# An adjacency built from one-hot products: the first two chunks' low one-hots made on the scalar engine, sixteen window ranges per register load, root products in two halves, and a scale chain spread over the attention loop

## The chip, the cores and the metric

The kernel runs as one program on one core of a Trainium2 chip. The metric is the device time of the whole program in microseconds (us), lower is better. TensorE multiplies matrices (PE in the rows, its weight loads are PEld), VectorE is DVE, ScalarE is ACT, GpSimd is POOL, and SyncE (SP) issues most of the transfers. Each engine has its own instruction stream. Its sequencer takes the instructions one by one, waits on semaphores, and does the register arithmetic.

## The reference

Two layers over a graph of 2500 nodes with 256 features and 80000 edges (sorted by destination). Each layer adds a graph convolution and an attention, then a feed-forward part. The parts that the change touches are the edge sums of layer 0 and the attention of layer 1:

```python
def _sage(x, src, dst, W_l, b_l, W_r):
    msg_sum = segment_sum(x[src], dst, N_NODES)
    cnt = segment_sum(ones, dst, N_NODES)
    return (msg_sum / maximum(cnt, 1.0)[:, None]) @ W_l.T + b_l + x @ W_r.T
h_fwd = _sage(x, src, dst, W_l_f, b_l_f, W_r_f)      # layer 0, both directions
h_bwd = _sage(x, dst, src, W_l_b, b_l_b, W_r_b)
...
# layer 1: linear attention with instance-normed k and v; its output joins x
```

## The kernel before

The kernel does the edge sums as dense matrix products. In `graph_stage` it first builds the adjacency matrix A (how many edges go from each source to each destination) out of one-hot vectors, and multiplies it with the projected features while it is being built.

The edges are cut into 625 **chunks** of 128. The destinations are cut into 80 **windows** of 32 nodes (`NW`), four to a **tile** of 128 (`XW`, index `x`; `t` is the tile, 0 to 19). Since the edges are sorted by destination, each window meets a run of chunks. The first two (`FQ`) have buffers of their own: `first_onehot_key` (`fok`, 640 columns a chunk) and `first_onehot_low` (`fol`, 128 columns a chunk). The rest come in **groups** of four (`Q`), with `onehot_key` (`ohk`) and `onehot_low` (`ohl`). Low windows have many edges, high ones few: window 0 takes 18 groups, windows 15 to 39 mostly 2, and from window 46 on each takes 1. How many groups a window has, and at which chunk it begins, is data. Both are packed into one integer of the row `ranges`, and each engine reads it into registers.

The work of one window by engine:

- DVE: the low one-hots of the first two chunks (L607), a register load of four windows' ranges every fourth window (L366, `fetch_tile`), two first keys (L611); then, for each group, four keys (L599) and two low one-hots for two chunks each (L603). A key waits until TensorE has used the one before it in the same buffer, four keys back.
- TensorE: four matmuls for the first chunks (L815), the same register load every fourth window (L366), then eight matmuls for each group (L804). After them come five transposes (L848) and five forward products (L857) for the tile before. In windows with `x == RT` (2) of tiles 0 to 5, eight matmuls follow for two tiles of the root product `x @ W_r` (`roots`, L762).
- ACT: a register load of the next window's range (L362), the source numbers shifted by the next window's offset (L671, `shift`), then the copies out of the PSUM banks: the last window's block of A turned (L697) and straight (L707), and in every fourth window the forward sums (L712).

Two windows' results have banks of their own (`x % 2`), so TensorE can't begin a window before ACT has copied the one two back. ACT may begin window `w`'s part only when DVE has made the low one-hots of all windows before it.

The other place is `linear_attention_stage`. It loops over 20 tiles. TensorE makes k and v (`kv`, L2871, two tiles ahead), ACT squares them, DVE turns the squares into a scale (L2979 to L2985) and scales k (L2988), and TensorE adds k and v into a 64x64 block for each head (`dots`, L2880). Ahead of this loop stands a short chain that scales the next stage's weights `sg_w`: ACT squares the weights (L2932), TensorE sums the squares (L2888), DVE takes the largest (L2968, L2969), ACT its root (L2935), and DVE scales (L2971 to L2975). GpSimd adds a bias to `X` in 20 instructions (L2857) from the stage's start.

## Time and profile before

| what | value |
|---|---|
| time, median of 3 | 1829.48 us (1828.7 to 1834.03) |
| the profiled execution's own time | 1833.38 us, its span 1831.6 us |
| TensorE busy | 1674.0 us, 91% |
| VectorE busy | 966.3 us, 53% |
| ScalarE busy | 669.4 us, 37% |
| granted TensorE clock, mean | 0.961 of full |
| edge windows (first L607 to last) | 47.9 to 434 us |
| linear attention stage | 1403 to 1543 us |

The span counts from the first to the last instruction. Shares of the span say little here, since stages with different limits follow each other. Each stage is read by itself.

### The profile page before, as it was taken

Reading aid. Unit: us, or ns where it says so; the run is one execution under the profiler, and the core shown is the slowest. Engines: PE = TensorE matmul, PEld = TensorE weight load, DVE = VectorE, ACT = ScalarE, POOL = GpSimd, SP = SyncE. Lnnn points to the kernel's source line nnn. Section 1 sums busy time; section 2 is a strip of 40 time slices with the busy share of each in tenths; the row PEclk is TensorE's granted clock in tenths of the full one; section 3 lists DMA queues with packets and bytes.
Section 4 is the critical chain, followed back from the end, with each engine's and each line's share of the span. In section 5 each row is a group of like instructions: output and inputs, shape, how many; then the busy total and the mean of one; then the engine's idle time right before and its main releaser. Section 6 shows DMA issues by size and latency. Waiting matters only on the chain. (4 is left out here: it accounts for less than half of the span.)

```text
span 1831.6 us, 31389 instructions
## 1 busy us (share of the span) xinstructions
PE 1674.0 (91%) x9423; PEld 1104.4 (60%) x9424; DVE 966.3 (53%) x2821; ACT 669.4 (37%) x1352; POOL 235.8 (13%) x290
## 2 busy tenths in 40 slices
PE   6889888987979899999799899999997989998998
PEld 5344555665747423333656799999955557644657
DVE  7888889887568664244511100000055874345862
ACT  3112444674024576665121344444321432201220
POOL 2100000001010003900044000000065000500002
PEclk8999999999989999999599999999998999999989
DMA  2000121225750000000513312211121002141001
GB/s 85 0 15 29 59 87 67 107 116 194 236 155 7 1 1 1 1 1 1 188 58 115 132 66 90 84 63 66 63 84 34 1 1 82 58 145 42 1 1 60
DMA packets 86409, 118.86 MB, mean 65 GB/s; under 512 B 6789, under 2 KB 72511, under 8 KB 86177
## 3 DMA queue, kind: packets, MB, share of 16 engines
q1 hardware_dynamic: 80992, 106.53, 17.2%
q0 software_dynamic: 3936, 10.37, 1.8%
q8 instruction: 55, 0.90, 0.2%
q10 hardware_dynamic: 1376, 0.66, 0.1%
q14 instruction: 50, 0.40, 0.1%
HBM read 70.66 MB, written 46.87 MB: 64 GB/s over the span
## 5 line engine op out<-in xcount | busy, mean ns | idle before, releaser
L804 PE MATMUL bank<-onehot_key,onehot_low 128*128 128x320 bf16 x1304 | 223.4, 303 | 38.2 <-DVE onehot_low L603 23.8
L599 DVE TENSOR_SCALAR onehot_key<-iota_keys,edge_keys 128x640 bf16<-128x640 f16 x652 | 231.5, 381 | 27.5 <-PE bank L804 22.7
L804 PEld LDWEIGHTS bank<-onehot_key,onehot_low 128*128 128x128 bf16 x1304 | 104.3, 99 | 147.9 <-DVE onehot_key L599 55.0
L2647 ACT ACTIVATE hidden<-bank,b_cols 128x128 f32<-128x128 f32 x344 | 126.4, 367 | 178.2 <-PE bank L2574 154.7
L2728 DVE TENSOR_TENSOR slot_columns<-bank,b_rows 128x256 f32 x43 | 18.3, 425 | 290.3 <-PE bank L2580 290.3
L2574 PEld LDWEIGHTS bank<-slot_columns,w 128*128 128x128 f32 x1376 | 162.8, 194 | 5.6 <-issue 3.4
L2574 PE MATMUL bank<-slot_columns,w 128*128 x1376 | 163.2, 278 | 3.2 <-issue 3.2
L2580 PE MATMUL bank<-w,hidden 128*128 128x256 f32 x688 | 155.6, 379 | 0.0
L671 ACT ACTIVATE edge_low_shifted<-edge_low,window_offset 128x631 f32 x81 | 66.7, 823 | 192.1 <-DVE onehot_low L603 191.2
L2580 PEld LDWEIGHTS bank<-w,hidden 128*128 128x128 f32 x688 | 127.4, 190 | 15.5
L1739 ACT ACTIVATE XT<-bank 128x512 f32<-128x512 f32 x160 | 84.3, 603 | 57.8 <-PE bank L1667 57.8
L603 DVE TENSOR_TENSOR onehot_low<-iota_low,edge_low_shifted 128x256 bf16<-128x256 f16 x326 | 95.1, 292 | 0.5
L1240 PE MATMUL bank<-sg_z,sg_strip 128*128 128x512 f16 x400 | 87.2, 379 | 1.5 <-POOL sg_z L1108 1.5
L2534 POOL DMA_INDIRECT slot_columns<-slot_results,slots x40 | 38.4, 960 | 355.9 <-SPq L2501 337.2
L2871 PE MATMUL bank<-w_kv,XT 128*128 128x512 f32 x160 | 74.0, 607 | 0.0
L2560 PE MATMUL bank<-w,hidden 128*128 128x256 f32 x320 | 70.4, 381 | 3.9 <-ACT hidden L2639 2.3
L1600 ACT ACTIVATE XT<-bank 128x512 f32<-128x512 f32 x120 | 63.0, 599 | 26.9 <-PE bank L1550 26.9
L2554 PE MATMUL bank<-XT,w 128*128 x160 | 71.3, 605 | 0.9 <-DVE slot_columns L2728 0.9
L2560 PEld LDWEIGHTS bank<-w,hidden 128*128 128x128 f32 x320 | 60.4, 190 | 16.0 <-ACT hidden L2639 4.8
L1240 PEld LDWEIGHTS bank<-sg_z,sg_strip 128*128 128x128 f16 x400 | 39.0, 98 | 47.9 <-POOL sg_z L1108 1.9
L611 DVE TENSOR_SCALAR first_onehot_key<-iota_keys,edge_keys 128x640 bf16<-128x640 f16 x160 | 55.0, 384 | 15.9 <-issue 15.9
L815 PE MATMUL bank<-first_onehot_key,first_onehot_low 128*128 128x320 bf16 x320 | 56.4, 298 | 5.3 <-DVE first_onehot_key L611 4.7
(517 smaller groups left out, 2745.4 us busy)
## 6 DMA issues: line engine op xcount, KB each, us to landing
AT_dram<-at_strip SPq DMA_DIRECT2D x20, 640.0 KB, 4.0
A_dram<-a_strips SPq DMA_DIRECT2D x20, 640.0 KB, 2.9
sg_strip<-AT_dram SPq DMA_DIRECT2D x20, 640.0 KB, 4.0
back_strip<-A_dram SPq DMA_DIRECT2D x24, 480.0 KB, 5.0
w<-in_L_ffn_W1p SPq DMA_DIRECT2D x8, 1024.0 KB, 5.3
w<-in_L_ffn_W2p SPq DMA_DIRECT2D x8, 1024.0 KB, 7.8
slot_rows<-ty_zero SPq DMA_DIRECT2D x1, 6144.0 KB, 24.5
slot_columns<-slot_rows SPq DMA_DIRECT2D x12, 512.0 KB, 8.7
```

The source lines that it names most:

```text
L599: dve.tensor_scalar(ohk[:, q, :], ioh[:, :], key[:, ds(chunk(n, offset, q), 1)], None, ALU.is_equal).then_inc(s_key[q], 1)
L603: dve.tensor_tensor(ohl[h][:, :, :], iow[:, :, :], spread(shifted[x % 2][:, ds(pair_of(n, even, q), 2)], 1, P), ALU.is_equal).then_inc(s_l ...
L671: act.activation(shifted[k][:, ds(odd, CHP)], lowc[:, :], ACT.Identity, bias=woff[:, ds(w, 1)]).then_inc(s_shift, 1)
L804: last = pe.matmul(bank[2 * (x % 2) + h][:, 0:HB], ohl[q // 2][:, :, q % 2], ohk[:, q, h * HB:(h + 1) * HB], start=False, stop=q == Q - 1, ...
L1240: last = pe.matmul(bank[5 + d % 3][:, :], strips[d % NBUF][:, s, :], zb[:, s, :], start=s == 0, stop=s == T - 1)
L1739: act.activation(FE[:, m % NF, :], bank[m % NS][:, :], ACT.Square).then_inc(p_fa, 1)
L2554: last = pe.matmul(bank[f % 6][:, :], w1[buf][:, c, f * P:(f + 1) * P], XT[:, c, ds(b * W, W)], start=c == 0, stop=c == CB - 1)
L2560: last = pe.matmul(bank[2 + j][:, 0:C], hid[:, f, j * P:(j + 1) * P], w2[buf][:, f, :], start=f == 0, stop=f == FB - 1)
L2574: last = pe.matmul(bank[f % 4][:, 0:P], w1[buf][:, c, f * P:(f + 1) * P], XS[:, t, c * P:(c + 1) * P], start=c == 0, stop=c == CB - 1)
L2580: last = pe.matmul(bank[4][:, 0:C], hid[:, f, 0:P], w2[buf][:, f, :], start=f == 0, stop=f == FB - 1)
L2647: act.activation(hid[:, f, 0:P], bank[f % 4][:, 0:P], ACT.Gelu, bias=b1[:, ds((e + 1) * FB + f, 1)]).then_inc(s_rg, 1)
L2871: last = pe.matmul(bank[KV[t % DEEP][half]][:, :], XT[:, c, t * P:(t + 1) * P], wc[:, c, half * I:(half + 1) * I], start=c == 0, stop=c == ...
```

## The change

- `fol` is made by ACT in four instructions for each window: the two chunks' columns of source numbers minus the window's offset (`first_columns`, L683, 128x2), a square of (number minus iota) for each chunk (L689, 128x128, two of them), and `Relu(1 - square)` over both (L692, 128x256). It is 1 where the numbers agree and 0 elsewhere. DVE's L607 is gone. `first_lows(w + 1)` stands at the end of ACT's window `w`. Its last instruction waits for the squares and for TensorE's use of window `w`'s `fol`.
- DVE and TensorE load sixteen ranges at a time (L371, `fetch_some`), at windows 0, 16, 32, 48 and 64.
- The root product of a tile pair is split: the first tile in the window with `x == 1`, the second in that with `x == 2`.
- In the attention stage the scale chain moves into the loop: ACT's squares after tile 2, TensorE's sums after `dots(3)`, DVE's steps after tiles 4, 5 and 8, and ACT's root after tile 7.

```diff
-                fol = sb(tmp, "first_onehot_low", [P, P, FQ], bf16)
+                fol = sb(tmp, "first_onehot_low", [P, FQ, P], bf16)
...
-                            if w % XW == 0:
-                                loaded.extend(fetch_tile(eng, w + 1))
+                            if w % FETCH == 0:
+                                loaded.extend(fetch_some(eng, w + 1))
...
                             dve.wait_ge(s_fused, w + 1)
-                            dve.tensor_tensor(fol[:, :, :], iow[:, :, :], spread(shifted[x % 2][:, ds(pair_of(before, even, -FQ), 2)], 1, P),
-                                              ALU.is_equal).then_inc(s_flow, 1)
                             packed = load_next()
...
+                        def first_columns(w, ranges):
+                            act.activation(fcol[:, :], lowc[:, ds(first_chunk(ranges[0], ranges[1]), FQ)], ACT.Identity, bias=woff[:, ds(w, 1)]).then_inc(s_fcol, 1)
+                        def first_lows(w):
+                            act.wait_ge(s_fcol, w + 1)
+                            for q in range(FQ):
+                                act.activation(fsq[:, q, :], iow[:, :, 0], ACT.Square, bias=fcol[:, q:q + 1], scale=-1.0).then_inc(s_fsq, 1)
+                            act.wait_ge(s_fsq, (w + 1) * FQ)
+                            act.wait_ge(s_fused, w + 1)
+                            act.activation(fol[:, :, :], fsq[:, :, :], ACT.Relu, bias=onesf[:, 0:1], scale=-1.0).then_inc(s_flow, 1)
...
                             shift(w + 1, (x + 1) % 2, following)
+                            first_columns(w + 1, following)
...
                                 halves(ZN - SOON + x)
+                            first_lows(w + 1)
...
-                            if x == RT and ROOTS + t < ZN:
-                                if t >= 2:
+                            if x in (RT - 1, RT) and ROOTS + t < ZN:
+                                if x < RT and t >= 2:
                                     pe.wait_ge(s_fc, t - 1)
-                                roots(ROOTS + t)
+                                root(ROOTS + t, x - (RT - 1))
...
                         for t in range(T):
                             if t + DEEP - 1 < T:
                                 kv(t + DEEP - 1)
                             dots(t)
+                            if t == 3:
+                                pe.wait_ge(s_wq, 1)
+                                for c in range(CB):
+                                    last = pe.matmul(bank[7][:, 0:C], onesf[:, :], wsq[:, c, :], start=c == 0, stop=c == CB - 1)
+                                last.then_inc(s_wn, 1)
```

On ACT, one window in the loop over pairs of tiles, before the change. The names in brackets are the semaphores that an instruction waits for: `chunk_used3` is TensorE's use of a window's last chunk, and `blocks_turned` its transposes.

```order
L362 ISA
L362 TENSOR_LOAD ranges
L370 REGISTER_ALU x2
L371 REGISTER_ALU
L677 REGISTER_ALU
L670 REGISTER_ALU [waits lows_ready1]
L671 ISA
L671 ACTIVATE edge_low_shifted<-edge_low,window_offset 128x631
L697 ACTIVATE at_strip<-bank 128x20x32 [waits chunk_used3]
L706 REGISTER_ALU
L707 ACTIVATE a_strips<-bank 128x640 [waits blocks_turned]
```

The same engine and loop in the changed kernel, from the new instructions at the end of one window to the next window's load and shift. `first_low_squares_ready` is set by the two instructions just ahead of the one that waits for it.

```order
L689 ACTIVATE first_low_squares<-iota_low,first_low_columns 128x128 [waits first_low_columns_ready]
L689 ACTIVATE first_low_squares<-iota_low,first_low_columns 128x128
L690 REGISTER_ALU
L692 ACTIVATE first_onehot_low<-first_low_squares,onesf 128x256 [waits first_chunks_used,first_low_squares_ready]
L367 ISA
L367 TENSOR_LOAD ranges
L375 REGISTER_ALU x2
L376 REGISTER_ALU
L698 REGISTER_ALU
L673 REGISTER_ALU [waits lows_ready1]
L674 ISA
L674 ACTIVATE edge_low_shifted<-edge_low,window_offset 128x631
```

With L683 behind the shift, four instructions have come into each window on ACT, and the register load of the next window now stands behind one that waits for the engine's own squares.

On DVE, the start of a window with a register load in the kernel before, first the end of the group loop:

```order
L613 COMPARE_AND_BRANCH
L594 REGISTER_ALU x2
L607 ISA [waits first_chunks_used,lows_shifted]
L607 TENSOR_TENSOR first_onehot_low<-iota_low,edge_low_shifted 128x256
L366 TENSOR_LOAD ranges
L611 ISA
L611 TENSOR_SCALAR first_onehot_key<-iota_keys,edge_keys 128x640
```

The same place in the changed kernel, at window 16:

```order
L616 COMPARE_AND_BRANCH
L599 REGISTER_ALU x2
L371 TENSOR_LOAD ranges [waits first_chunks_used,lows_shifted]
L614 ISA
L614 TENSOR_SCALAR first_onehot_key<-iota_keys,edge_keys 128x640
```

The load still stands ahead of the first keys. It now brings sixteen values, and no one-hot is made beside it.

## Rows read from the trace of the kernel before

**Rows 1.** Windows of time (stretch, its length, busy us of PE, PEld, DVE, ACT, POOL with counts, clock, DMA share, GB/s)

```profile
47.89:206.70 158.81, 138.53 (x833) 70.61 (x831) 138.06 (x493) 37.58 (x61) 6.16 (x6) 0.97 0.05 21
...
316.71:434.10 117.39, 104.94 (x896) 75.67 (x894) 103.42 (x373) 84.95 (x130) 0.00 (x0) 1.00 0.28 114
```

**Rows 2.** Waits of the edge stage, and L599's group from 316.71 us on

```profile
DVE onehot_key L599 <- PE bank L804: 22.7, 18, 4.0
...
L599 DVE TENSOR_SCALAR onehot_key<-iota_keys,edge_keys 128x640 bf16<-128x640 f16 x169 | 60.9, 381 | 2.2 <-PE bank L804 0.6 <-issue 0.5
```

**Rows 3.** Timeline of DVE (start, us, instruction, count [idle before it and releaser])

```profile
255.90 0.29 DVE L607 TENSOR_TENSOR first_onehot_low<-iota_low,edge_low_shifted 128x256 bf16<-128x256 f16 x1
256.10 0.68 DVE L611 TENSOR_SCALAR first_onehot_key<-iota_keys,edge_keys 128x640 bf16<-128x640 f16 x2
...
259.98 0.29 DVE L607 TENSOR_TENSOR first_onehot_low<-iota_low,edge_low_shifted 128x256 bf16<-128x256 f16 x1
...
386.22 0.28 DVE L607 TENSOR_TENSOR first_onehot_low<-iota_low,edge_low_shifted 128x256 bf16<-128x256 f16 x1
...
388.68 0.28 DVE L607 TENSOR_TENSOR first_onehot_low<-iota_low,edge_low_shifted 128x256 bf16<-128x256 f16 x1
...
392.13 0.28 DVE L607 TENSOR_TENSOR first_onehot_low<-iota_low,edge_low_shifted 128x256 bf16<-128x256 f16 x1
...
394.99 0.29 DVE L607 TENSOR_TENSOR first_onehot_low<-iota_low,edge_low_shifted 128x256 bf16<-128x256 f16 x1 [0.31 <-PE bank L815]
```

**Rows 4.** Timeline of PE in the same windows

```profile
386.78 0.44 PE L848 MATMUL bank<-identh,at_strip 128*128 128x128 f16 x5
...
389.24 0.44 PE L848 MATMUL bank<-identh,at_strip 128*128 128x128 f16 x5
...
...
392.06 1.11 PE L804 MATMUL bank<-onehot_key,onehot_low 128*128 128x320 bf16 x7 [1.05 <-DVE onehot_low L603]
```

**Rows 5.** Timeline of ACT in the same windows

```profile
384.52 0.70 ACT L697 ACTIVATE at_strip<-bank 128x640 f16<-128x640 f32 x1 [0.16 <-PE bank L804]
...
389.04 0.82 ACT L671 ACTIVATE edge_low_shifted<-edge_low,window_offset 128x631 f32 x1 [0.76 <-DVE onehot_low L603]
389.76 0.68 ACT L697 ACTIVATE at_strip<-bank 128x640 f16<-128x640 f32 x1
390.35 0.69 ACT L707 ACTIVATE a_strips<-bank 128x640 f16<-128x640 f16 x1
```

**Rows 6.** The group of instructions nearest to the new squares

```profile
L2647 ACT ACTIVATE hidden<-bank,b_cols 128x128 f32<-128x128 f32 x344 | 126.4, 367 | 178.2 <-PE bank L2574 154.7
```

**Rows 7.** ACT's sequencer by line, 384.4:385.1, then 388.1:389.2 (ns min/median/max, first and last start)

```profile
L706 ACTq ALU_OP  x1: 38/38/38, 384.5 to 384.5; - x1
...
L362 ACTq FUSED_REGOPS  x1: 46/46/46, 388.1 to 388.1; - x1
```

**Rows 8.** Register loads by line: of four values (L366), of one (L362)

```profile
L366 DVEq TENSOR_LOAD <-ranges x20: 959/964/989, 47.9 to 422.8; - x20
L366 PEldq TENSOR_LOAD <-ranges x20: 997/1007/1845, 50.4 to 424.6; - x20
...
L362 ACTq TENSOR_LOAD <-ranges x92: 272/282/875, 45.9 to 432.8; - x92
```

**Rows 9.** The window of time behind window 4's register load

```profile
128.30:135.10 6.80, 6.71 (x28) 3.70 (x28) 5.10 (x18) 0.00 (x0) 0.00 (x0) 0.58 0.00 0
```

**Rows 10.** The attention stage's start, by line and from the timeline

```profile
L2857 POOL TENSOR_TENSOR X<-X,la_out_bias x20: 728/734/742, 1403.8 to 1416.8; 128x256 f32<-128x256 f32 x20
...
L2969 DVE TENSOR_SCALAR sg_scale<-sg_scale x1: 2632/2632/2632, 1414.9 to 1414.9; 128x3 f32<-128x3 f32 x1
...
1413.36 1.03 PE L2888 MATMUL bank<-sg_wl_squares,onesf 128*128 128x256 f32 x4
...
1420.16 0.17 DVE L2980 TENSOR_SCALAR la_ss<-la_ss 128x16 f32<-128x16 f32 x1
...
1422.69 2.08 PE L2880 MATMUL bank<-la_k,la_v 128*128 128x128 f32 x8 [4.87 <-DVE la_k L2988]
```

More of the change, by code:

```diff
@@ L362, in fetch, with fetch_some @@
                     return eng.value_load(par[0:1, ds(w, 1)])
-                def fetch_tile(eng, w):
-                    return list(nc.values_load_multi_w_load_instructions(par[0:1, w:w + XW], engines=[eng.engine])[1])
+                def fetch_some(eng, w):
+                    return list(nc.values_load_multi_w_load_instructions(par[0:1, w:w + FETCH], engines=[eng.engine])[1])
                 def parts(eng, packed):
@@ L671, in shift, with first_chunk @@
                             act.activation(shifted[k][:, ds(odd, CHP)], lowc[:, :], ACT.Identity, bias=woff[:, ds(w, 1)]).then_inc(s_shift, 1)
+                        def first_chunk(before, offset):
+                            return nc.s_assert_within(before * Q + offset - (FQ + BIAS), 0, CHP - FQ, skip_runtime_bounds_check_because=
+                                                      "the first chunk that reaches a window is one of the CH chunks")
+                        def first_columns(w, ranges):
[7 more added lines that the diff above has]
+                            act.activation(fol[:, :, :], fsq[:, :, :], ACT.Relu, bias=onesf[:, 0:1], scale=-1.0).then_inc(s_flow, 1)
                         def window(i, k, x, ranges, load_next):
@@ L712, in forward_copy @@
                             act.activation(AG[:, ds(t, 1), :].rearrange("p t c -> p (t c)"), bank[6 + k][:, 0:FW], ACT.Copy).then_inc(s_fc, 1)
-                        shift(0, 0, load(act, 0))
+                        opening = load(act, 0)
+                        shift(0, 0, opening)
+                        first_columns(0, opening)
+                        first_lows(0)
                         halves(2 * early + 1)
@@ L754, in product, with root @@
                             last.then_inc(s_z, 1)
+                        def root(j, i):
+                            t = 2 * j + i
+                            for c in range(CB):
+                                last = pe.matmul(bank[6 + j % 2][:, i * 2 * P:(i + 1) * 2 * P], XT[:, c, t * P:(t + 1) * P], wr[:, c, :], start=c == 0, stop=c == CB - 1)
+                            if i == 1:
+                                last.then_inc(s_rp, 1)
                         def roots(j):
@@ L759, in roots @@
                             for i in range(2):
-                                t = 2 * j + i
-                                for c in range(CB):
-                                    last = pe.matmul(bank[6 + j % 2][:, i * 2 * P:(i + 1) * 2 * P], XT[:, c, t * P:(t + 1) * P], wr[:, c, :], start=c == 0, stop=c == CB - 1)
-                            last.then_inc(s_rp, 1)
+                                root(j, i)
                         pe.wait_ge(s_gm, 1)
@@ L814, in window @@
                                 for h in range(2):
-                                    last = pe.matmul(bank[2 * (x % 2) + h][:, 0:HB], fol[:, :, q], fok[:, q, h * HB:(h + 1) * HB],
+                                    last = pe.matmul(bank[2 * (x % 2) + h][:, 0:HB], fol[:, q, :], fok[:, q, h * HB:(h + 1) * HB],
                                                      start=q == 0, stop=False, skip_group_check=True)
@@ L2885, in _ @@
                             kv(t)
-                        pe.wait_ge(s_wq, 1)
-                        for c in range(CB):
-                            last = pe.matmul(bank[7][:, 0:C], onesf[:, :], wsq[:, c, :], start=c == 0, stop=c == CB - 1)
-                        last.then_inc(s_wn, 1)
                         for t in range(T):
@@ L2893, in _ @@
                             dots(t)
+                            if t == 3:
+                                pe.wait_ge(s_wq, 1)
+                                for c in range(CB):
+                                    last = pe.matmul(bank[7][:, 0:C], onesf[:, :], wsq[:, c, :], start=c == 0, stop=c == CB - 1)
+                                last.then_inc(s_wn, 1)
                         pe.wait_ge(s_dt, 1)
@@ L2988, in _ @@
                             dve.tensor_tensor(by_head(K[k][:, :]), by_head(bank[KV[t % DEEP][0]][:, :]), spread(ss[k][:, 2, 0:Hh], 2, Dh), ALU.mult).then_inc(s_k, 1)
+                            if t == 4:
+                                dve.wait_ge(s_wq, 2)
+                                dve.tensor_reduce(gz[:, 1:2], gq[:, 0, :], AX.X, ALU.max)
+                                dve.tensor_reduce(gz[:, 2:3], gq[:, 1, :], AX.X, ALU.add)
+                            if t == 5:
+                                dve.wait_ge(s_wn, 1)
+                                st.then(dve.tensor_reduce(gz[:, 0:1], bank[7][:, 0:C], AX.X, ALU.max))
+                                dve.tensor_scalar(gz[:, 0:3], gz[:, 0:3], 1e-20, None, ALU.max).then_inc(s_gm, 1)
+                            if t == 8:
+                                dve.wait_ge(s_gr, 1)
+                                st.then(dve.scalar_tensor_tensor(out=gz[:, 6:7], in0=gz[:, 4:5], scalar=float(C) ** 0.5, in1=gz[:, 5:6], op0=ALU.mult, op1=ALU.add))
+                                st.then(dve.scalar_tensor_tensor(out=gz[:, 6:7], in0=gz[:, 6:7], scalar=1.0 / (HALF_SCALE * C ** 0.5), in1=gz[:, 3:4], op0=ALU.mult, op1=ALU.mult))
+                                st.then(dve.reciprocal(gz[:, 7:8], gz[:, 6:7]))
+                                dve.tensor_scalar(sg_sf[:, :], indeg[:, :], gz[:, 6:7], None, ALU.mult)
+                                dve.tensor_scalar(sg_w[:, :, 0:C], sg_w[:, :, 0:C], gz[:, 7:8], None, ALU.mult)
                         dve.wait_ge(s_use, T)
```

29 lines of the change are left out of this document (12 added, 17 removed).

## The prediction, made before the changed kernel was run

> **What bounds the kernel now.** I read the stages one by one, since the page's shares average over stages with different limits. The change touches two, the edge windows and the attention stage.
>
> The edge windows first, in three stretches [rows 1]. The first holds windows 0 to 15 (18 groups down to 2), the second windows 16 to 39 (two groups each, one of them a single), the third windows 40 to 79. L599's count says how many groups the third has: 169 / 4 = 42, so 38 windows of one group and 2 of two [rows 2]. TensorE and the vector engine are busy nearly 90% in the first and the third alike, while the scalar engine climbs from 24% to 72%. That is the column to watch.
>
> The vector engine's timeline gives its price of a window from one L607 to the next [rows 3]. Two groups take 259.98 - 255.90 = 4.08 us and one group takes 388.68 - 386.22 = 2.46, so a group is 1.6 and the rest 0.86. Nothing is idle in these; the vector engine sets the pace where a window has two groups or more. With one group TensorE needs the same 2.46 (389.24 - 386.78) and has no gap either [rows 4]. Window 64 has a register load and takes 392.13 - 388.68 = 3.45 [rows 3], and TensorE stands idle for 1.05 us before its groups [rows 4]. The window behind it takes 2.86, another 0.4 too much, waiting for TensorE. So a load costs about 1.4; with the register steps of a two-group window I take 1.5 everywhere.
>
> **L607 leaves the vector engine.** L607 takes 0.29, but L611 starts 0.20 behind it [rows 3]. So each window with two groups or more shrinks by 0.20, to 3.88. In one-group windows TensorE still needs 2.46. In windows with a load nothing is saved, for the load runs beside L607. In root windows the vector engine already waits for TensorE (part of the 22.7 us of rows 2), so I count one 0.20 for each pair.
>
> **The same work on the scalar engine.** This is the term that decides. The engine starts the next instruction about 0.10 before one ends [rows 5]: 389.04 to 389.76 is 0.72 for the shift, 389.76 to 390.35 is 0.59 for a copy. The new squares are nearest to L2647, also 128x128 with a column as bias: 0.367 [rows 6]. L683 (128x2) has no row. The shift has 631 columns and a bias and takes 0.82, L2647 has 128 and takes 0.367, so the line through both gives about 0.25 for two columns, 0.15 to the next start. Then the chain that the order shows: `Relu` waits for the second square, so that one counts to its end. While an instruction waits, the sequencer stands: L697 waited for TensorE until 384.52 [rows 5], and the register instruction behind it ran at 384.5, not before [rows 7]. So the next window's register load begins when `Relu` does. From the load's first instruction (388.1, rows 7) to the shift it leads to (389.04, rows 5) are 0.90. One window then takes
>
> 0.72 shift + 0.15 columns + 0.59 + 0.59 copies + 0.27 first square + 0.37 second + 0.05 semaphore + 0.90 = **3.65 us**,
>
> where before the load ran beside the copies. Two-group windows (3.88) still hide it, one-group windows (2.46) don't: `fol` comes too late for TensorE, and the scalar engine becomes the bound there.
>
> By the Trainium skill's "ScalarE: Activation LUTs", What ACT_TABLE_LOAD costs, an instruction with a column operand takes about 280 ns plus 0.833 ns an element and overlaps the next by 93; by that L683 and the squares cost 0.08 more in a window, and the third stretch 3 us more.
>
> Third stretch: 40 x 3.65 = 146.0, less 2.0 for a lag that the double buffers take up before TensorE waits, plus 5.0 for two register loads (below): 149.0 against 117.4 [rows 1], **+31.6**.
>
> **Sixteen ranges a load.** The trace has loads of four (0.96 on the vector engine, 1.01 on TensorE) and of one (0.28, on the scalar engine) [rows 8]. The slope between them is 0.23 to 0.24 a value, if the fixed part is alike; then sixteen cost 2.8 more on each engine. Below, nothing more. The two loads of a window stand in a row: TensorE waits for the first keys behind the vector engine's, then does its own. So a bigger load costs 0 to 5.6 more; I take 4.6, nearer to the slope.
>
> By the Trainium skill's "Runtime: NRT & Kernel Launch", Instruction fetch mechanics, such a load takes about 200 ns a register even in bulk, which would make it 4.8; no row shows sixteen.
>
> Five loads stay, fifteen go. Window 4's load took 1.85 on TensorE [rows 8], and behind it the clock was 0.58 for 6.8 us [rows 9], so TensorE idle for such a time falls to its lower level (1.2 GHz). I price one such fall at 2.5: 6.8 x 0.42 = 2.9 of work lost, less some slack. The long loads at 16 and 32 leave gaps longer still, so each should bring a fall.
>
> - First stretch: loads at 4, 8, 12 gone, -(3 x 1.5 + 2.5) = -7.0; L607 7 x 0.20 + 4 x 0.20 = -2.2; window 0's bigger load +4.6. Sum **-4.6**.
> - Second: 18 x 0.20 + 2 x 0.20 = -4.0; four loads gone, -6.0; two bigger ones 2 x (4.6 + 2.5) = +14.2. Sum **+4.2**.
> - Third: at 48 and 64 the scalar engine's pace hides the vector engine's load, but TensorE's 3.4 and the slow clock behind it hold back the copies; 2.5 each, the 5.0 above.
>
> **Halved root products.** The same eight matmuls in two pieces. A two-group window has little slack left at its end, and L607's 0.20 takes that. I count nothing beyond the 0.20 for each pair. Bounds: a loss of nothing, a gain of 0.9 for each of six tiles, 5 in all, if one half hides.
>
> **The scale chain.** Before, the scalar engine's first square waited for this chain, so TensorE idled 4.87 us before `dots(0)` at 1422.69 [rows 10]. With the chain gone the first squares wait for tile 0's k and v alone. TensorE has these well before 1413.36, when L2888 follows tile 1's [rows 10]. But L2969, a tensor_scalar of three columns, took 2.63 us and ended when GpSimd's 20 additions did, at 1417.5 [rows 10]. The loop's own first tensor_scalar (L2980) would now come inside these additions, and be held in the same way to 1417.5. It ended at 1420.3 before, so `dots(0)` comes 2.8 earlier. L2888's four matmul passes lay in cover ahead of that stall; now they stand in a loop that TensorE paces, +0.9. **-1.9**. If nothing holds L2980, the stall goes, and a clock fall's 2.5 behind it too: 4.9 + 2.5 - 0.9, so -6.5. The spread steps themselves lie beside TensorE's matmuls; if they didn't, they would cost what they do now, some 2 us.
>
> **Sum.** -4.6 + 4.2 + 31.6 - 1.9 = +29.3 on the profiled execution's 1833.4. It stood 3.9 above the median, 1829.5, so the forecast is 1829.5 + 29.3 = **1859**. Differences under 0.3% (5.5 us) can't be told from none here.
>
> **The rivals.**
>
> - *The scalar engine's register load overlaps.* If its sequencer runs past `Relu`'s wait, a window costs 3.65 - 0.90 + 0.37 = 3.12 (0.37 is `Relu` to the next start, its 256 columns on the same line, less 0.10). Third stretch 127.8, total +8.1: 1838. Against it: rows 5 and 7. Chance 0.13.
> - *The scalar engine keeps up: faster.* If its window stays under TensorE's 2.46, the third stretch is 38 x 2.46 + 2 x 3.88 + 2 x 6.1 = 113.4, -4.0; total -6.3: 1823. For it: the engine was idle 28% of that stretch. Against it: start to start, without any wait or load, the instructions already sum to 0.72 + 0.15 + 0.59 + 0.59 + 0.27 + 0.27 + 0.37 = 2.96. It decides at a window of 2.93 us: below it the kernel is faster. Chance 0.10.
> - *Sixteen load as fast as four.* Then -4.6, -14.2 and -5.0 off the three stretches: 1835, at the edge of no change. Chance 0.10.
> - *The clock falls in the third stretch.* TensorE would idle a third of each window. At half speed it needs 4.9 a window instead of the 3.65; for half of the windows 20 x 1.25 = +25: 1884. Against it: it ran at 1.00 in the whole third stretch with a 1.05 gap every fourth window. Chance 0.08.
>
> The forecast has 0.54, and 0.05 is left. Its own range is 1846 to 1874. The range for 8 in 10 reaches down to the two mild rivals and up past the page's prices: **1833 to 1877**. Faster 0.12, within 0.3% 0.10, slower 0.78.
>
> **What would show it.** From about window 46 on, `edge_low_shifted` every 3.5 to 3.8 us on the scalar engine with no idle time but about 0.5 ahead of it, and TensorE's L845 waiting for L692. Two-group windows of 3.9 us. Loads of 3 to 4 us on both engines, and a clock fall behind windows 16 and 32. L2980 taking some 6 us once. The forecast is wrong if the one-group windows stay near 2.5 us, or if the scalar engine idles before its shift waiting for the vector engine there.

## The result

| kernel | median of its runs, us |
|---|---|
| before | 1829.09 (1827.12 to 1834.03, 4 runs) |
| changed | 1877.33 (1875.93 to 1878.94, 4 runs) |

The changed kernel is slower: ratio 1.0264, 95% interval 1.0245 to 1.0283, or +48.2 us. The forecast was +29 and 1859, its range ended at 1877.0. The direction and the place were right, the size was not. Beside one group of the experiments the kernel before once took 4150 us; the ratios leave that execution out, the medians don't.

### The profile page after: what moved, and what is told of

Its sections match the earlier page's. It is cut to its first block and busy times, and to the rows that moved or that the text cites. A ratio compares the mean times of both kernels' runs of the same rounds, so it can differ in the third digit from the quotient of the medians.

```text
span 1874.2 us, 31819 instructions
## 1 busy us (share of the span) xinstructions
PE 1676.9 (89%) x9423; PEld 1102.8 (59%) x9424; DVE 951.5 (51%) x2741; ACT 770.8 (41%) x1676; POOL 236.5 (13%) x290
## 3 DMA queue, kind: packets, MB, share of 16 engines
q1 hardware_dynamic: 80992, 106.53, 16.8%
```

## The profile after

The three edge stretches of the changed kernel, in the columns of [rows 1] (stretch, its length, busy us of PE, PEld, DVE, ACT and POOL with counts, clock, DMA share, GB/s):

```profile
47.89:204.60 156.71, 138.12 (x840) 70.19 (x840) 133.32 (x477) 57.93 (x125) 4.81 (x4) 0.97 0.06 25
204.60:319.64 115.04, 99.43 (x716) 61.77 (x716) 93.42 (x331) 78.92 (x170) 0.00 (x0) 0.91 0.16 65
319.64:481.40 161.76, 111.89 (x889) 75.06 (x888) 97.46 (x333) 130.72 (x283) 0.00 (x0) 0.94 0.20 82
```

They took 158.81, 110 and 117.39 before. So the first is 2.1 shorter, the second 5 longer and the third 44.4 longer (forecast: -4.6, +4.2, +31.6). In the third the scalar engine went from 84.95 to 130.72 us of work, 81% of the stretch, and no other engine is above 70%. The granted clock is no longer 1.00 there, and part of the 44.4 belongs to the two long register loads at windows 48 and 64; the experiments take the two apart.

The scalar engine's timeline in one-group windows, where [rows 5] showed it waiting for the vector engine:

```profile
397.76 0.69 ACT L689 ACTIVATE first_low_squares<-iota_low,first_low_columns 128x128 f32<-128x128 f16 x2
398.48 0.51 ACT L692 ACTIVATE first_onehot_low<-first_low_squares,onesf 128x256 bf16<-128x256 f32 x1
399.32 0.82 ACT L674 ACTIVATE edge_low_shifted<-edge_low,window_offset 128x631 f32 x1 [0.33 <-issue]
400.05 0.28 ACT L683 ACTIVATE first_low_columns<-edge_low,window_offset 128x2 f32 x1
400.24 0.68 ACT L720 ACTIVATE at_strip<-bank 128x640 f16<-128x640 f32 x1
400.82 0.69 ACT L730 ACTIVATE a_strips<-bank 128x640 f16<-128x640 f16 x1
401.40 0.68 ACT L689 ACTIVATE first_low_squares<-iota_low,first_low_columns 128x128 f32<-128x128 f16 x2
```

From one pair of squares to the next are 401.40 - 397.76 = 3.64 us. The only idle time is the 0.33 ahead of the shift, put down to "issue": the register load that stands behind `Relu`. TensorE in the same windows (its timeline) has the gap that was not in [rows 4], once in each window:

```profile
399.09 0.70 PE L845 MATMUL bank<-first_onehot_key,first_onehot_low 128*128 128x320 bf16 x4 [1.02 <-issue]
399.63 1.25 PE L834 MATMUL bank<-onehot_key,onehot_low 128*128 128x320 bf16 x8
...
402.73 0.70 PE L845 MATMUL bank<-first_onehot_key,first_onehot_low 128*128 128x320 bf16 x4 [1.02 <-issue]
```

These rows name no releaser, but the matmuls start 0.10 behind the end of `Relu` (398.48 + 0.51 = 398.99, and 399.09). In the kernel with the one-hots alone, below, a row of the same gap names it:

```profile
368.25 0.70 PE L839 MATMUL bank<-first_onehot_key,first_onehot_low 128*128 128x320 bf16 x4 [1.01 <-ACT first_onehot_low L690]
```

The register loads by line (ns min/median/max, first and last start), the answer to [rows 8]:

```profile
L371 DVEq TENSOR_LOAD <-ranges x5: 3604/3619/4367, 43.7 to 415.2; - x5
L371 PEldq TENSOR_LOAD <-ranges x5: 3826/5145/6053, 48.4 to 419.8; - x5
...
L367 ACTq TENSOR_LOAD <-ranges x92: 273/282/858, 42.0 to 484.5; - x92
```

What one such pair does, in TensorE's timeline at window 48, and the window of time behind it (columns as above):

```profile
348.51 0.71 PE L887 MATMUL bank<-z_halves,at_strip 128*128 128x257 f16 x5
352.08 0.70 PE L845 MATMUL bank<-first_onehot_key,first_onehot_low 128*128 128x320 bf16 x4 [2.86 <-DVE first_onehot_key L614]
358.86 2.29 PE L834 MATMUL bank<-onehot_key,onehot_low 128*128 128x320 bf16 x8 [6.07 <-issue]
```

```profile
354.40:364.60 10.20, 5.75 (x26) 3.67 (x27) 2.51 (x9) 3.86 (x9) 0.00 (x0) 0.50 0.31 125
```

TensorE waits 2.86 us for keys that stand behind the vector engine's load, then 6.07 for its own. The granted clock is at its lower level (1.2 GHz) for 10.2 us, and eight matmuls take 2.29 instead of 1.25. Behind each of the four loads at windows 16, 32, 48 and 64 the clock is at 0.50 for 10.2 us, where before there was the one of 6.8 behind window 4's [rows 9] and none behind the later ones. In window 0 it is 10.2 us instead of 3.4.

## The experiments

Times in the headings are medians, and the kernel before beside them is that of the same chip. Where a stretch is named, the first runs from the first keys of window 0 to those of window 16, the second to window 40, and the third to window 79 (before: 158.76, 109.91 and 114.08 us in its profiled execution). Line numbers are each kernel's own. The ratios are those on record, not the quotients of the medians.

Stages that no edit touches don't take the same time in every profiled execution. From the last shift of the edge stage to GpSimd's first addition in the attention stage it is 970.0 to 972.2 us in eleven of the fourteen kernels, and 975.9 to 976.2 in three (the chain alone, the halves alone, and the load ahead of `Relu`). So a difference of medians can hold some 6 us that no step of the edit explains, and between kernels that ran on different chips the ratios are the better measure.

### The four parts, one at a time

**One-hots alone** (loads of four, whole roots, old chain):

> The kernel before with the first chunks' low one-hots alone moved to the scalar engine; loads of four ranges, whole root products and the old scale chain stay. Theory (the scalar engine is the bound in one-group windows, at the 3.64 to 3.9 us that the changed kernel's trace shows, mean 3.79): third stretch 40 x 3.79 = 151.6 less 2 of lag, so about 150 against 117.4, and nothing saved in the two-group windows, since these stayed at 4.1 us in the changed kernel: about +32. Rival, the prediction's own sum: 3.65 a window and 0.20 saved in each window of two or more groups: 144 - 117.4 - 6.2 = +20 to +27. Rival, the long loads and the slow clock behind them made the one-group windows slow, and the one-hots alone cost 3.12 us a window: third stretch 125 to 128, +8 to +10.

Measured: 1858.0 against 1828.5, ratio 1.0158 (1.0138 to 1.0179), **+29.5**. The stretches in its profile:

```profile
45.82:199.40 153.58, 134.98 (x837) 68.84 (x838) 134.70 (x477) 59.04 (x128) 6.02 (x5) 1.00 0.06 22
199.40:307.94 108.54, 97.97 (x730) 59.40 (x729) 93.28 (x330) 81.04 (x176) 0.00 (x0) 1.00 0.18 74
307.94:455.11 147.17, 110.18 (x866) 74.00 (x865) 95.08 (x325) 127.81 (x279) 0.00 (x0) 0.97 0.23 91
```

The third went from 114.08 to 147.17, with three clock falls of only 3.4 us each. So the scalar engine alone makes the one-group windows slow, and the rival of slow clocks falls. The second gave back 1.4 of the 4.0 that the prediction had for L607.

**Sixteen ranges alone** (`par[0:1, w:w + 16]` at every sixteenth window):

> The kernel before with sixteen ranges per register load alone. Theory (a load of sixteen takes 3.6 us on the vector engine and 3.8 to 6 on TensorE, in a row, with the clock at half for 10 us behind it: some 9.8 us for each window with one): first stretch -2, second 2 x 9.8 - 4 x 1.5 - 2 x 1.5 = about +11, third the same two loads and ten removed, about +6: +12 to +16 in all. Rival, the prediction's prices (4.6 for the load, 2.5 for the clock): first -2.4, second +8.2, third +2.2: +8. Rival, the load is dear only beside the new scalar-engine work: -15 to -25.

Measured: 1844.25, ratio 1.0079 (1.0061 to 1.0098), **+15.8**, the top of the theory. It is dear by itself: the second stretch took 116.58 (109.91 before) and the third 121.57 (114.08).

**Scale chain alone:**

> The kernel before with the scale chain alone spread over the attention loop; nothing in the edge stage. Theory (the small operations of the vector engine wait about one GpSimd instruction each, 0.6 to 0.8 us, and are not held to the end of the 20 additions, so the stall ahead of the first dots goes and the slow clock behind it too): -6. Rival, the prediction: the first of them is held until GpSimd is done, -1.9. Rival, the gain seen in the changed kernel came from another start of the stage: 0.

Measured: 1821.18, ratio 0.9955 (0.9941 to 0.997), **-7.3**. Its vector engine's timeline and TensorE's at the start of the stage:

```profile
1413.15 4.66 DVE L2971 TENSOR_SCALAR la_ss<-la_ss 128x16 f32<-128x16 f32 x1
```

```profile
1420.16 1.16 PE L2880 MATMUL bank<-la_k,la_v 128*128 128x128 f32 x8 [2.55 <-DVE la_k L2979]
```

The loop's first tensor_scalar was held for 4.66 us, to the end of GpSimd's additions, as the prediction had it. `dots(0)` came 16.7 us behind the stage's start instead of 19.5, the 2.8 of the prediction. But its matmuls took 1.16 instead of 2.08 [rows 10], so the slow clock behind the stall went although 2.55 of the stall stayed, and the loop to the last `dots` took 80.8 instead of 82.8 to 83.3. My theory (nothing is held) had the size and the wrong reason.

The two explained parts, 2.8 and some 2, are 5 of the 7.3. The two profiled executions lie further apart than the medians: from GpSimd's first addition to the end it is 427.8 us before and 415.2 here, since TensorE's clock was low for 47.7 us of it before and for 24.6 here, and two thirds of the difference are at the end of the attention loop and behind it, where nothing was changed.

**Halved roots alone:**

> The kernel before with the root product of a tile pair alone split over the windows x = 1 and x = 2. Prediction: nothing. Rival, one half hides in its window's slack: up to -0.9 for each of six tiles, -5. Rival, two windows now each wait longer than one did, since each half ends behind the window's own products and the vector engine has slack for neither: +1 to +3.

Measured: 1826.21, ratio 0.9983 (0.997 to 0.9995), -2.3, under what can be told here. In its trace windows 17 to 20 take 19.65 us, 19.60 before: window 18 is 0.86 longer, for the half that came, and window 19 is 0.86 shorter, for the half that left. The product wasn't hidden anywhere.

### Are the parts' costs additive?

The changed kernel with `FETCH = 4`:

> The changed kernel with loads of four ranges again (the constant 16 set to 4), all else as changed. The four parts alone measured +29.5 (one-hots), +15.8 (sixteen), -7.3 (chain) and -2.3 (halves), 35.7 together, and the whole +48.2. Theory A (the long load costs more beside the scalar engine's one-hots than alone): this one is the sum of three parts, 1828.5 + 29.5 - 7.3 - 2.3 = 1848.4, and sixteen cost 28 here. Theory B (the parts' sum falls short because the halved roots gain nothing and the single profiles differ by chance): 1851 to 1854. Theory C (the one-hots cost more when the roots are halved): 1860.

Measured: 1853.19 (1843.66 to 1858.9), ratio 1.0126 (1.009 to 1.0163); the runs of both kernels were spread wider on this chip, so the times alone don't choose between A and B. The profile does. Its third stretch:

```profile
306.94:454.03 147.09, 110.10 (x866) 74.05 (x865) 95.05 (x325) 127.80 (x279) 0.00 (x0) 0.97 0.23 91
```

That is the 147.17 of the one-hots alone. The first two stretches, where the halved roots lie, take 262.0 us together, and 262.1 with the one-hots alone. So the halves add nothing, and C falls.

With sixteen the third stretch was 159.39. From the first keys to the last shift this kernel takes 411.6 us and the changed one 434.0, and the changed one's first keys come at 47.6 instead of 45.0, for window 0's load stands ahead of them. So sixteen cost 22.4 + 2.6 = 25 us here. The same measure gives 16.8 for sixteen alone (396.7 us instead of 382.5, and the 2.6), and the median 15.8. So A holds, with 25 instead of its 28. That the ratios say the same (1.0264 and 1.0126 are 25 us apart) is weaker, since this kernel's interval is 13 us wide.

Of the 8.2 between 25 and 16.8, 4.8 lie in the third stretch. There the removed loads give back less. In the kernel with sixteen alone, windows 47 to 50 take 20.2 us instead of 4 x 2.46, so a long load costs 10.4; the stretch grew by only 7.5 (121.57 - 114.08), so the ten loads of four that went gave back 2 x 10.4 - 7.5 = 13.3. In the changed kernel the stretch grew by 12.3 for the two, 6.2 each, and the loads of four gave nothing back: the scalar engine's pace had hidden them (eight of its windows take 30.92 us with them and 30.93 without). Another 3.6 lie in the first stretch, where the profile of the kernel before has the clock fall of [rows 9].

### Is it the sequencer that stands at Relu?

On the one-hots alone, the scalar engine's register load moved ahead of `Relu`, one window earlier:

```diff
-                            following = load_next()
                             act.wait_ge(s_low[1], before + 1)
...
+                            after_next = load_next()
                             first_lows(w + 1)
-                            return following
+                            return after_next
```

The cut leaves out the loop around it, which now loads two ranges at the start of every pair of tiles.

> The kernel with the one-hots alone on the scalar engine, and its register load of the window after next standing ahead of Relu and of the squares instead of behind Relu. Theory (the sequencer stands at Relu until the second square has ended, so that the load's 0.83 to 0.90 us lie bare in every one-group window; the load now lies beside the copies, and Relu's 0.37 to the next start is left): window 3.64 - 0.83 + 0.37 = 3.2, mean 3.3 with the forward copies, third stretch about 20 shorter than with the one-hots alone, 1838. Rival (the engine's own busy time is the bound and the load was hidden anyway): no change, 1858. Either way over the 1828.5 of before, since 3.2 is over TensorE's 2.46.

Measured: 1846.65, ratio 1.0075 (1.0054 to 1.0097), 11.4 less than with the load behind `Relu`, on another chip; the ratios (1.0158 there) are 15 us apart. The third stretch went from 147.17 to 131.38. The scalar engine's timeline:

```profile
371.55 0.69 ACT L688 ACTIVATE first_low_squares<-iota_low,first_low_columns 128x128 f32<-128x128 f16 x2
372.27 0.51 ACT L691 ACTIVATE first_onehot_low<-first_low_squares,onesf 128x256 bf16<-128x256 f32 x1
372.68 0.81 ACT L673 ACTIVATE edge_low_shifted<-edge_low,window_offset 128x631 f32 x1
...
375.88 0.81 ACT L673 ACTIVATE edge_low_shifted<-edge_low,window_offset 128x631 f32 x1
```

The shift follows `Relu` after 0.41 instead of 0.84, without idle time, and a window takes 375.88 - 372.68 = 3.20. So the bare load was worth 0.44 a plain window, as the theory had it. The size missed: the stretch fell by 15.8 and not by 20. The window at the start of each pair of tiles gained nothing, since two loads stand in a row there and 1.16 us stay idle ahead of its shift. The median fell by less than the stretch did; this profiled execution has 5.7 us more in the stages between (above). 3.2 is still over TensorE's 2.46: with this order too the one-hots are too much for this engine.

### What a long load costs

The vector engine's load behind its first keys instead of ahead of them, with the scale chain spread:

```diff
-                            packed = load_next()
                             for q in range(FQ):
                                 dve.tensor_scalar(fok[:, q, :], ...).then_inc(s_fkey[q], 1)
+                            packed = load_next()
```

> The kernel before with the scale chain spread, and the vector engine's load of four ranges standing behind the two first keys instead of ahead of them. Theory (the two engines' loads stand in a row now, since TensorE waits for the first keys behind the vector engine's load and then does its own; behind the keys they run side by side): each of 20 loads saves 0.7 to 1.0 of its 1.5, so -14 to -20 against the chain alone, 1821 - 17 = 1804. Rival (TensorE's own load and the register steps behind it set the gap): the vector engine's load is exposed behind the keys as it was ahead of them, -0 to -3, 1820.

Measured: 1800.17 against 1833.66, ratio 0.9823 (0.9795 to 0.9852). That is **21 less than the chain alone** (1821.18), measured on another chip; by the ratios it is 24. The forecast was 14 to 20, and the medians reach past it by luck. In the profiled executions the edge windows, from the first keys to the last shift, went from 380.8 to 366.9 us, so 13.9 lie where the edit is, and 5.8 of the rest in the stages between (976.1 and 970.3), which it doesn't touch. Of the 13.9, 2.1 are window 0, whose 3.4 us of slow clock are gone. TensorE's timeline at window 64 shows what is left of a pair of loads:

```profile
373.71 0.70 PE L815 MATMUL bank<-first_onehot_key,first_onehot_low 128*128 128x320 bf16 x4
374.92 1.45 PE L804 MATMUL bank<-onehot_key,onehot_low 128*128 128x320 bf16 x8 [0.50 <-DVE onehot_low L603]
```

0.50 of idle TensorE, where [rows 4] had 1.05 and a wait for the first keys too. The loads stood in a row, and side by side a part of their cost goes: in the third stretch four windows with one load take 10.7 to 11.1 us instead of 11.3 to 11.5, and 9.9 to 10.1 where no load stands (in the kernels with sixteen). So a load costs some 0.8 instead of 1.35. The 0.5 to 0.7 saved is under the 0.7 to 1.0 of the theory.

One range a load, in every window, behind the keys:

> As the one before, but one range per load, a load in every window. Theory (a load of one takes 0.28 us and lies beside the second first key on the vector engine and beside the first matmuls on TensorE): as the one before or up to 10 better, 1795 to 1804. Rival (every window's start is already full for the sequencers, since two-group windows stayed at 4.07 us when an instruction left them): 80 x 0.28 = 22 appear, 14 to 20 are saved, 1823 to 1830.

Measured: 1811.09, ratio 0.988 (0.9847 to 0.9913), 11 more than with four. In the profiled executions 7.4 lie in the edge windows (374.3 us against 366.9 from the first keys to the last shift), and 8.4 behind the first `dots`, where the code is the same and the clock was low for 38.5 us instead of 17.1. Two-group windows took 4.35 instead of 4.08. The theory was too hopeful and the rival too gloomy: a load in each window costs some 0.27 where the vector engine paces.

Which of the two loads brings the clock down? Sixteen on one engine only:

> The kernel before, but the vector engine alone loads sixteen ranges at a time; TensorE keeps its loads of four. Sixteen on both cost +15.8. A load of four costs about 1.5 now, some 0.8 of it the vector engine's part and 0.7 TensorE's. Theory (the vector engine's 3.6 us alone leave TensorE idle for long enough that the clock falls to half for 10 us, worth 2.7): -15 x 0.8 + 5 x 2.7 + 5 x 2.7 = +15, so 1843, with four or five such falls in the edge windows. Rival (the fall needs both loads in a row): -12 + 13.5 = +1.5, 1830, no fall behind them.

> The mirror of the run before: TensorE alone loads sixteen ranges, the vector engine four. Theory (its own 3.8 us are enough for the clock to fall): -15 x 0.7 + 5 x 2.8 + 5 x 2.7 = +17, 1845. Rival (it needs both in a row): -10.5 + 14 = +3.5, 1832.

Measured: 1839.08 (ratio 1.0061, 1.0038 to 1.0083) and 1848.15 (1.0104, 1.0087 to 1.0122). The loads by line, of the first kernel and of the second:

```profile
L366 DVEq TENSOR_LOAD <-ranges x5: 3625/5071/5661, 43.8 to 391.5; - x5
```

```profile
L366 PEldq TENSOR_LOAD <-ranges x5: 3824/5832/5900, 47.6 to 401.9; - x5
```

The theories (1843 and 1845) were near. Either load alone brings a clock fall at each of windows 16, 32, 48 and 64, of 3.4 to 6.8 us, not the 10 that the theory had. So the rivals, by which it takes both, fall. TensorE's own load alone costs more than both together do: 402.4 us from the first keys to the last shift, against 396.7 with sixteen on both. It took 5.8 to 5.9 here and mostly 3.8 there, and the vector engine's fifteen other loads of four stay here; which of the two counts for how much wasn't tried.

Sixteen and eight ranges, side by side:

> Scale chain spread, and on the vector engine the load behind the first keys, so that the two engines' loads run side by side, with sixteen ranges a load; the same kernel with four took 1800.2. Theory (each load of sixteen leaves TensorE idle for its own 3.8 us, and the clock falls behind it): 5 x (3.8 + 2.7) - 20 x 0.95 = +13.5, 1814. Rival (side by side the gap is too short for a fall): 5 x 3.8 - 19 = 0, 1800. Rival (the loads' price is not their length, but the wait in a row): 1790.

> As the run before with eight ranges a load. Theory (time goes with the number of values, and about 1.9 us of idle TensorE bring no fall): 10 x 1.9 = 19, as with four: 1800, within 3. Rival (a fall behind each): +27, 1827.

Measured: 1815.72 (ratio 0.9928, 0.991 to 0.9947) and 1806.33 (0.9887, 0.9864 to 0.991; its runs lie between 1797.23 and 1811.25). The third stretch of each, of sixteen and of eight:

```profile
315.93:433.03 117.10, 105.85 (x875) 76.91 (x875) 99.31 (x365) 82.41 (x128) 0.00 (x0) 0.94 0.28 114
```

```profile
302.02:411.40 109.38, 101.84 (x875) 73.00 (x875) 98.55 (x364) 81.75 (x128) 0.00 (x0) 1.00 0.30 122
```

Eight took 109.38, and four 109.35. So up to eight the time goes with the number of values and the clock stays at 1.00. With sixteen the two loads of the stretch cost 7.7 us more than the five of eight. Two things are in that: the loads took 5.8 to 5.9 us on TensorE instead of two times 1.93, and the clock was low for 13.7 us. The rival by which the wait in a row is the whole price falls. The profile with sixteen is of the slowest of its five executions (1826.55 us), the one with eight of the fastest of its four, so the whole spans aren't compared here; what spreads the eight's times doesn't show in the one profile.

## Why the prediction was right or wrong

By parts, the forecast had +20.4 for the one-hots (26.6 less the 6.2 of L607), +10.8 for sixteen ranges, -1.9 for the chain and nothing for the halves. The runs show +29.5, +25, -7.3 and nothing. So the mechanism was right, and two terms carry the miss: the price of a long register load, most of all the step by which the scalar engine hides it, and the one-hots, whose mean window was taken too short and whose 0.20 a window off the vector engine mostly didn't come.

**Right: what becomes the bound.** The prediction made the scalar engine the bound of the one-group windows, at 3.65 a window (its printed terms add up to 3.64). Plain windows take 3.64, and the terms hold nearly one by one. Shift to next start 0.73, columns 0.19, copies 0.58 each, both squares and the semaphore 0.72, and the load chain 0.84. By the Trainium skill's "ScalarE: Activation LUTs", What ACT_TABLE_LOAD costs, the columns and the squares were to take 0.28 and 0.39, and the trace has 0.28 and 0.39; it didn't make the window longer, since the chain was 0.06 shorter than taken. Both rivals under it (3.12, and an engine that keeps up) fell; 3.20 is what the first takes when it is built.

**Mis-sized: "40 x 3.65 = 146.0, less 2.0".** It priced every window as a plain one. The scalar engine's shifts at the end of the stretch show what was left out:

```profile
450.67 0.82 ACT L674 ACTIVATE edge_low_shifted<-edge_low,window_offset 128x631 f32 x1 [0.33 <-DVE onehot_low L608]
...
455.12 0.82 ACT L674 ACTIVATE edge_low_shifted<-edge_low,window_offset 128x631 f32 x1 [1.15 <-issue]
...
459.00 0.82 ACT L674 ACTIVATE edge_low_shifted<-edge_low,window_offset 128x631 f32 x1 [0.57 <-issue]
...
462.91 0.82 ACT L674 ACTIVATE edge_low_shifted<-edge_low,window_offset 128x631 f32 x1 [0.33 <-issue]
...
466.55 0.83 ACT L674 ACTIVATE edge_low_shifted<-edge_low,window_offset 128x631 f32 x1 [0.33 <-issue]
...
470.18 0.82 ACT L674 ACTIVATE edge_low_shifted<-edge_low,window_offset 128x631 f32 x1 [0.32 <-issue]
...
474.05 0.82 ACT L674 ACTIVATE edge_low_shifted<-edge_low,window_offset 128x631 f32 x1 [0.57 <-issue]
...
476.14 0.38 ACT L735 ACTIVATE forward_sums<-bank 128x257 f32 x1
...
477.96 0.82 ACT L674 ACTIVATE edge_low_shifted<-edge_low,window_offset 128x631 f32 x1 [0.32 <-issue]
...
481.59 0.82 ACT L674 ACTIVATE edge_low_shifted<-edge_low,window_offset 128x631 f32 x1 [0.33 <-issue]
```

Three of the eight windows take 3.63 or 3.64. The two with the forward copy, named among ACT's work in the kernel's description and not in the sum, take 3.91. Two with a longer register load take 3.87 or 3.88 (0.57 idle instead of 0.33). And one takes 4.45: the loop of the scalar engine goes over pairs of tiles and loads a range of its own at each start, so two loads stand in a row there (at 453.9 and 454.4), and 1.15 us are idle ahead of the shift. So eight windows take 30.92, or 3.87 a window instead of 3.65. Against that, the lag that the double buffers take up was more than the 2.0 of the sum: 39 windows at 3.87 are 150.8, and the stretch from key to key took 147.17. The term measured +33.1 (147.17 - 114.08) where +26.6 were forecast.

**Wrong: "L607 leaves the vector engine, 3.88".** Two-group windows stayed at 4.1. The vector engine's timeline in the changed kernel, one window from its first keys on:

```profile
258.50 0.67 DVE L614 TENSOR_SCALAR first_onehot_key<-iota_keys,edge_keys 128x640 bf16<-128x640 f16 x2
...
260.25 0.28 DVE L608 TENSOR_TENSOR onehot_low<-iota_low,edge_low_shifted 128x256 bf16<-128x256 f16 x1
260.46 0.90 DVE L604 TENSOR_SCALAR onehot_key<-iota_keys,edge_keys 128x640 bf16<-128x640 f16 x2
...
262.57 0.38 DVE L614 TENSOR_SCALAR first_onehot_key<-iota_keys,edge_keys 128x640 bf16<-128x640 f16 x1
```

262.57 - 258.50 = 4.07. Two keys take 0.68 elsewhere and 0.90 at 260.46, where the second comes later: a key waits for TensorE's use of the one four back, and the saved 0.20 stands there. The sum of these waits is no measure of it:

```profile
DVE onehot_key L604 <- PE bank L834: 44.8, 28, 7.0
```

It was 22.7 before [rows 2], but 34.5 with sixteen ranges alone and 24.3 with the one-hots alone, so most of the growth goes with the long loads.

TensorE in the same window, in its timeline:

```profile
261.71 1.45 PE L834 MATMUL bank<-onehot_key,onehot_low 128*128 128x320 bf16 x8 [0.17 <-DVE onehot_low L608]
```

It waits for the vector engine as the vector engine waits for it. So "the vector engine sets the pace" was too simple: taking 0.20 off one of the two left the loop through both at 4.07. Which step of that loop would have to shrink wasn't tried. The one-hots alone gave 1.4 of the forecast's 4.0 in the second stretch, and 1.1 of its 2.2 in the first behind window 0 (121.2 us instead of the 122.3 with the chain alone). Window 0 is 2.1 to 2.6 shorter too, but that is hardly the 0.20. In the three kernels with L607 and the load ahead of the keys the clock is low for 3.4 us there (34.6 to 35.0 us), and in the three with the one-hots moved and loads of four it isn't (32.4 to 32.5). The kernel with the load behind the keys keeps L607, has no such fall and takes 32.65.

**Wrong: the sixteen-range load.** The forecast had +10.8 for it (-2.4, +8.2 and +5.0); it cost 15.8 alone and 25 in the changed kernel. Cut at the vector engine's loads of windows 0 and 16 and at the first keys of window 40, these 25 are +2.9, +9.8 and +12.3. Three things were too low. The load itself: "0 to 5.6 more, I take 4.6" was 3.6 - 0.96 on one engine and 3.8 - 1.0 on the other at the least, 5.4, so the slope held; on top came up to 2.2 us more, on one engine or both, in four of the five windows. The Trainium skill's "Runtime: NRT & Kernel Launch", Instruction fetch mechanics, has about 200 ns a register, for loads that the page places in HBM and not, as the row `ranges` here, in the core's own memory; the shortest loads show 225 and 239 ns. The clock: 10.2 us at half instead of the 6.8 that was the pattern. And the step that failed by most, "at 48 and 64 the scalar engine's pace hides the vector engine's load" at "2.5 each": they cost 159.39 - 147.09 = 12.3 for the two. The scalar engine, meant to be the cover, itself waited for TensorE (at 361.27 in its timeline):

```profile
361.27 0.70 ACT L720 ACTIVATE at_strip<-bank 128x640 f16<-128x640 f32 x1 [5.09 <-PE bank L834]
```

The removed loads of four gave nothing back there, which the prediction had seen, and the two long ones cost over twice what it took. The 2.5 for window 4's clock fall was no saving. None of the six other kernels with loads of four on both engines has that fall, and two of them have the same idle times. In the kernel with the chain alone:

```profile
123.76 0.70 PE L815 MATMUL bank<-first_onehot_key,first_onehot_low 128*128 128x320 bf16 x4 [1.03 <-DVE first_onehot_key L611]
126.35 1.25 PE L804 MATMUL bank<-onehot_key,onehot_low 128*128 128x320 bf16 x8 [1.90 <-issue]
```

Eight matmuls in 1.25 us are at the full clock. So "TensorE idle for such a time falls to its lower level" was read from a single execution, and the same idle time doesn't always bring it. Behind loads of sixteen the fall came at windows 16, 32, 48 and 64 in all five kernels that have one.

**The scale chain: -1.9 was -7.3.** The hold by GpSimd was right where the chain stood alone, and in the changed kernel it didn't come: L3001 took 0.62, and five of the small operations behind it 0.64 to 0.80 each. Of the seven kernels with the new chain four have the hold (3.6 to 4.7 us) and three don't. `dots(0)` came 15.2 behind the stage's start there. Why one kernel is held and the other not wasn't tried. The +0.9 for L2888 didn't show, and the slow clock behind the stall, which the prediction let go only without a hold, went in both. So the step that failed is that the slow clock hangs on the hold; the stall's 2.8 and the loop's 2 are shown. The rest is put down to the clock further on, without proof. One part of it is a fall of 10.2 us some 363 to 370 us behind the stage's start: all seven profiled kernels with the old chain have it, of the seven with the new chain three. What it depends on is open.

**Halved roots: nothing**, as forecast.

Put together from the runs: 29.5 for the one-hots, 25 for sixteen ranges, -7.3 for the chain and nothing for the halves are 47.2, and 48.2 were measured. The 25 come from the changed kernel itself; the same three parts, each alone, give 38.0, and 9 of the 10 between are what the long loads cost more beside the one-hots. The version that the runs point to is the kernel before with the chain spread and the vector engine's load of four behind its first keys, 1800.2 us, 1.8% under before.

## What to carry to other kernels

Before work goes to an engine that looks idle, sum its instructions start to start over one round of the loop, the ones that come only every fourth time too, and let a register load that stands behind a wait count bare, with the second load at a loop's turn; compare the sum with the pace of the stage where the windows are shortest. Taking work off the engine that seems to set the pace gives little if another loop of waits is as long, and stalls that a slower engine hides give nothing back when they go. Two engines that each load registers should do it side by side (here 0.5 to 0.7 us less for each pair of loads), and in portions short enough that the clock stays up. And before a difference of medians is put down to an edit, compare the stages that the edit doesn't touch.

## What was unexpected in the hardware

- A load of sixteen registers took 3.6 us on the vector engine and 3.8 on TensorE at the least, but in most windows one of the two, or both, took 4.3 to 6.05. What lengthens them wasn't tried. Loads of eight took 1.84 to 1.86 and 1.93 to 2.07.
- At windows 16, 32, 48 and 64 one long load (4.5 to 5.9 us), or two side by side, brought 3.4 to 6.8 us at the lower clock, and two in a row 10.2. Shorter idle times of 1.03 and 1.90 us brought a fall in one kernel and none in two others. With loads of eight side by side the granted clock was 1.00 in all edge windows.
- Most vector-engine operations on 16 columns took 0.17 us alone and 0.62 to 0.80 while GpSimd added. In four kernels one of them took 3.6 to 4.7, to the end of GpSimd's additions.
- While the scalar engine's sequencer stood at `Relu`, the register load behind it didn't run: it started 0.08 us behind `Relu`. With the load moved ahead no idle time was left, and a plain window went from 3.64 to 3.20 us.
